# Two-layer convolution and scan network on one Trainium2 core: extra columns that hold the last value of both scans in layer 1

## The chip, the cores and the metric

One core of one Trainium2 chip runs the whole program. The metric is the device time of one execution in microseconds (us).

## The reference, cut to what matters

The input is 32 images of 96 channels and 56 x 56 pixels, in fp32. Layer 0 is a 7 x 7 depthwise convolution, a layer norm over the channels, two dense products with a GELU between them, and a residual sum. Layer 1, where the change is, is a 5 x 5 depthwise convolution followed by a selective scan along the 3136 pixels of each image:

```
x = silu(conv(x) + conv_b);  xs = x.reshape(B, C, L)
x_dbl = einsum('kd,bdl->bkl', x_proj_w, xs)
dts, Bs, Cs = x_dbl[:, :R], x_dbl[:, R:R+N], x_dbl[:, R+N:]
delta = softplus(einsum('dr,brl->bdl', dt_w, dts) + dt_b)
log_dA = maximum(delta * A, log(EPS));  P = exp(cumsum(log_dA))
dB_u = delta * Bs * xs
hs = P * cumsum(dB_u / maximum(P, EPS))
y = einsum('bdnl,bnl->bdl', hs, Cs) + xs * Ds
```

N is 4 (states), R is 6 and EPS is 1e-9.

## The kernel before, in words

The two layers run one after the other, each as a loop over 8 groups of 4 images, and x1_dram holds what goes from one to the other. Each layer is written as one queue of instructions per engine, and the engines are tied by semaphores alone. So every engine does its work in the order of its own queue. The last group of a layer stands as code of its own behind the loop.

In layer 1 the 384 rows of a group (4 images x 96 channels) are three tiles of 128 partitions, and the 3136 pixels are BANDS = 7 bands of BT = 448 columns. A band has STEPS = 12 steps: 3 tiles x 4 states, and a group S = 84 steps. The steps are counted through the group, so that step s is state s % 4 of tile s % 12 // 4 in band s // 12. Bands are counted from 0 here, and the groups too. What happens in one step s:

- ScalarE (ACT) makes d_a = exp(max(delta * A, log EPS)) in two passes, clip_a (L1205) and exp_a (L1211), five steps ahead (DA_LEAD).
- VectorE (DVE) runs a scan with products over d_a, which gives 1 / P in the tile ps_q in PSUM but for its bound (scan_q, L1099; the first value is 1/EPS), cuts it at 1 and multiplies it by u in place (gate, L1115), and runs the scan of the state, h = d_a * h + ps_q (scan_h, L1126). ps_q has two banks and h has six slots (H_SLOTS).
- GpSimd (POOL) makes u = dxs * b_rows (times_b, L1023) three steps ahead, and h = h * c_rows in place (times_c, L1036) one step behind. dxs = delta * xs is made three times per band (times_x, L1011).
- TensorE (PE) adds the four products of a tile in PSUM with matmuls by the identity (add_y, L1348), two steps behind; scan_h waits until the slot that it writes has been added.

A band goes on where the one before it ended, separately in each of the 12 steps. So DVE copies the last column of ps_q to a column of q_last after each scan_q (keep_q, L1107), POOL copies the last column of h to a column of h_last before it overwrites h (L1033), and both scans take that column as their first value 12 steps later. The last band of a group (band 6) has no such copies, since nothing follows it.

```
def keep_q(g, s):
    if b + 1 < BANDS:
        dve.wait_ge(q_done, g * S + s + 1)
        nc.vector.tensor_copy(q_last[:, j:j + 1], ps_q[s % 2][:, BT - 1:BT]).then_inc(q_kept, 1)
```

DVE's queue in step s is keep_q(s), gate(s), at three places of a band sum_delta (L1089), scan_q(s + 1), scan_h(s). sum_delta forms delta of the next band's tile t from ps_prep and z_log at steps 7, 9 and 11 of a band (SUM_AT); it waits for ACT's softplus parts, of which the last is the Ln at L1187.

PE and ACT also prepare the next group's input, spread over the steps by a table (`schedule`, `backs`): transposes of the image (L1293), the banded convolution (L1300), and transposes back to rows of channels (L1313) in bursts at steps 0, 35, 60 and 72, which ACT's SiLU follows (L1169, between two loads of its table of functions). ACT takes all of it out of PSUM: the parts win and conv at L1162. PE waits in its queue for ACT to free the two banks. For the next band PE further has project (L1322) at j = 0 and 1 and delta_rows (L1335) at j = 3, 5 and 7, where j is the step within the band. The last group has none of the preparation. SyncE (SP) issues all DMAs in one queue, among them those of b_rows and c_rows for each band.

Of the kernel before, what the change touches and what calls it, by code (L numbers as in the profile page):

```python
# [81 lines left out]
H_SLOTS = 6  # L82
Y_LAG = 2
# [631 lines left out]
def layer1(nc, groups, x1, t2, consts, out):  # L715
# [4 lines left out]
    with ExitStack() as ctx:  # L720
# [41 lines left out]
        ps_q = [pb(f"ps_q{i}") for i in range(2)]  # L762
        ps_y = [pb(f"ps_y{i}") for i in range(Y_SLOTS)]
        no_q = ps_q[0][:, BT:BT + 1]
# [36 lines left out]
        PREPARED = 4 + TILES + 1  # L801
        S = BANDS * STEPS
        RUNS = BANDS * TILES
        KEPT = (BANDS - 1) * STEPS

# [189 lines left out]
        def _(pool):  # L995
            nc.gpsimd.memset(zeros[:, :], 0.0).then_inc(prepared, 1)
            nc.gpsimd.memset(q_first[:, :], float(np.float32(1) / np.float32(EPS))).then_inc(prepared, 1)
            nc.gpsimd.memset(log_eps[:, 0:1], -LOG_EPS).then_inc(prepared, 1)
            for k in range(Y_SLOTS):
                pool.sem_inc(y_stored[k], 16)  # L1000
# [70 lines left out]
        def _(dve):  # L1071
# [20 lines left out]
            def scan_q(g, s):  # L1092
                b, j = s // STEPS, s % STEPS
                dve.wait_ge(d_a_ready, g * S + s + 1)
                dve.wait_ge(h_done, g * S + max(s, 1))
                if s > 1:
                    dve.wait_ge(q_kept, g * KEPT + min(s - 1, KEPT))  # L1097
                first = q_first[:, 0:1] if b == 0 else q_last[:, j:j + 1]
                nc.vector.tensor_tensor_scan(ps_q[s % 2][:, 0:BT], d_a[s % DA_SLOTS][:, :],  # L1099
                                             no_q.broadcast_to([128, BT]), first,  # L1100
                                             ALU.mult, ALU.add).then_inc(q_done, 1)

            def keep_q(g, s):
                b, j = s // STEPS, s % STEPS
                if b + 1 < BANDS:
                    dve.wait_ge(q_done, g * S + s + 1)
                    nc.vector.tensor_copy(q_last[:, j:j + 1], ps_q[s % 2][:, BT - 1:BT]).then_inc(q_kept, 1)  # L1107

            def gate(g, s):
                b = s // STEPS  # L1110
                dve.wait_ge(q_done, g * S + s + 1)
                if b + 1 < BANDS:
                    dve.wait_ge(q_kept, g * KEPT + s + 1)
                dve.wait_ge(u_done, g * S + s + 1)
                nc.vector.scalar_tensor_tensor(ps_q[s % 2][:, 0:BT], ps_q[s % 2][:, 0:BT], 1.0, u[s % U_SLOTS][:, :],  # L1115
                                               ALU.min, ALU.mult).then_inc(gated, 1)

            def scan_h(g, s):
# [31 lines left out]
        def _(act):  # L1150
# [47 lines left out]
            def clip_a(g, s, first=False):  # L1198
# [70 lines left out]
        def _(pe):  # L1269
# [68 lines left out]
            def add_y(g, s):  # L1338
# [9 lines left out]
                nc.tensor.matmul(total, ident[:, :], h[s % H_SLOTS][:, :],  # L1348
# [119 lines left out]
```

## Time and profile before

| | |
|---|---|
| median of 3 runs | 4020.88 us (4011.57 to 4022.5) |
| the profiled execution's own time | 4020.36 us |
| its span in the trace | 4018.6 us |
| mean granted clock of TensorE | 0.928 |
| first scan of h in layer 1 starts at | 1959.5 us |

Layer 0 takes about the first half of the span; layer 1 holds DVE and POOL at nine tenths in most slices. A row of the trace gives the start in us from the beginning of the span, the duration in us, engine, line, operation, output <- input, shape and count. In brackets stands how long the engine was idle before it and which instruction ended that, as far as the semaphores show. A row's duration is longer than the distance to the next row on the same engine, since the end of one instruction lies over the start of the next; distances between starts tell what an instruction costs.

### The profile page before, as it was taken

How to read it: one execution, taken by the hardware profiler on the slowest of the kernel's cores; microseconds unless marked ns; L12 is line 12 of the kernel's file. 1: busy time of each engine (PE TensorE's matmuls, PEld its weight loads, DVE VectorE, ACT ScalarE, POOL GpSimd, SP SyncE). 2: the span in 40 equal slices, each digit the busy share in tenths (PEclk: the TensorE clock that was granted, in tenths of full speed). 3: DMA queues.
4: the chain of work that ended last, by engine and by line, in shares of the span. 5: the costliest groups of instructions: out<-in, count | busy, mean ns of one | idle time of the engine just before them, and what ended most of it. 6: DMA issues, size and time to landing. Idle time of an engine off the chain costs nothing. (4 is left out here: it accounts for less than half of the span.)

```text
span 4018.6 us, 72697 instructions
## 1 busy us (share of the span) xinstructions
PE 3650.8 (91%) x22358; PEld 2646.6 (66%) x22358; DVE 3106.0 (77%) x4416; ACT 2571.1 (64%) x4292; POOL 2575.8 (64%) x2672
## 2 busy tenths in 40 slices
PE   6999999999999999997899998998989989899776
PEld 6888787979787887877565564664646646466322
DVE  3675758475756667570499998999989989989999
ACT  1463728172735546274688787787778878777754
POOL 0352717162634536270488888888979889888988
PEclk9999999999999999998799898998989989989877
DMA  7546473747465554428565564655546646465222
GB/s 225 170 138 204 104 250 95 251 102 234 109 200 149 164 181 125 149 76 181 130 177 143 162 170 124 172 152 147 164 127 181 169 125 173 129 168 158 86 75 60
DMA packets 383746, 612.84 MB, mean 153 GB/s; under 512 B 199967, under 2 KB 324152, under 8 KB 383048
## 3 DMA queue, kind: packets, MB, share of 16 engines
q1 hardware_dynamic: 383336, 607.74, 53.5%
q8 instruction: 213, 3.49, 0.4%
q14 instruction: 197, 1.61, 0.1%
HBM read 527.35 MB, written 80.28 MB: 151 GB/s over the span
## 5 line engine op out<-in xcount | busy, mean ns | idle before, releaser
L321 POOL TENSOR_TENSOR h_low<-act_h,h_high 128x448 fp32r<-128x448 f32 x448 | 598.0, 1354 | 724.1 <-ACT h_high L520 723.9
L515 ACT ACTIVATE act_h<-ps_up,b 128x448 f32<-128x448 f32 x672 | 408.7, 635 | 728.5 <-PE ps_up L633 728.2
L1348 PE MATMUL ps_y<-h,ident 128*128 128x448 f32 x1344 | 727.1, 629 | 144.3 <-POOL h L1036 113.1
L1036 POOL TENSOR_TENSOR h<-h,c_rows 128x448 f32<-128x448 f32 x672 | 763.7, 1136 | 51.2 <-DVE h L1126 5.7
L1023 POOL TENSOR_TENSOR u<-dxs,b_rows 128x448 f32<-128x448 f32 x672 | 764.5, 1138 | 27.9 <-DVE ps_q L1115 16.8
L1099 DVE TENSOR_TENSOR_SCAN ps_q<-d_a,q_last,ps_q 128x448 f32<-128x448 f32 x576 | 659.5, 1145 | 0.0
L1126 DVE TENSOR_TENSOR_SCAN h<-d_a,h_last,ps_q 128x448 f32<-128x448 f32 x576 | 645.3, 1120 | 0.0
L1300 PEld LDWEIGHTS ps_front<-win,taps 120*112 120x112 f32 x4608 | 540.5, 188 | 149.2 <-issue 147.2
L606 PE MATMUL ps_stage<-win,taps 124*112 124x112 f32 x6144 | 608.3, 261 | 2.7 <-DVE w_low L368 2.7
L606 PEld LDWEIGHTS ps_stage<-win,taps 124*112 124x112 f32 x6144 | 608.1, 178 | 3.2 <-DVE w_low L368 2.8
L1205 ACT ACTIVATE d_a<-delta,log_eps,a_neg 128x448 f32<-128x448 f32 x672 | 503.3, 750 | 114.0 <-DVE h L1126 58.5
L1300 PE MATMUL ps_front<-win,taps 120*112 120x112 f32 x4608 | 543.9, 271 | 5.5 <-ACT win L1162 3.7
L1348 PEld LDWEIGHTS ps_y<-h,ident 128*128 128x128 f32 x1344 | 238.2, 209 | 412.9 <-POOL h L1036 260.3
L1115 DVE SCALAR_TENSOR_TENSOR ps_q<-ps_q,u 128x448 f32<-128x448 f32 x672 | 422.2, 628 | 59.8 <-POOL u L1023 36.1
L426 DVE TENSOR_TENSOR conv<-ps_stage,bias_row 112x448 f32<-112x448 f32 x192 | 179.7, 936 | 350.8 <-PE ps_stage L606 350.8
L1211 ACT ACTIVATE d_a<-d_a 128x448 f32<-128x448 f32 x672 | 387.6, 577 | 8.3
L315 POOL TENSOR_TENSOR ln_rstd<-ln_var,minus_half 112x7 f32<-112x7 f32 x128 | 202.8, 1585 | 285.0 <-DVE ln_var L403 280.9
L1162 ACT ACTIVATE conv<-ps_front 112x448 f32<-112x448 f32 x192 | 181.8, 947 | 214.1 <-PE ps_front L1300 214.1
L629 PE MATMUL ps_up<-hn_high,w_high 96*128 96x448 f32 x672 | 258.4, 385 | 40.3 <-DVE hn_low L413 26.8
L1293 PEld LDWEIGHTS ps_front<-ident,x1pad 32*120 32x120 f32 x2880 | 197.2, 143 | 142.4 <-issue 140.8
L1011 POOL TENSOR_TENSOR dxs<-delta,xs 128x448 f32<-128x448 f32 x168 | 191.1, 1138 | 137.0 <-DVE delta L1089 137.0
L1162 ACT ACTIVATE win<-ps_front 120x480 f32<-120x480 f32 x192 | 203.6, 1062 | 79.9 <-PE ps_front L1293 77.5
(81 smaller groups left out, 6212.6 us busy)
## 6 DMA issues: line engine op xcount, KB each, us to landing
taps<-in_t_dram SPq DMA_DIRECT2D x192, 896.0 KB, 5.0
taps<-in_t_dram SPq DMA_DIRECT2D x192, 672.0 KB, 4.7
b_rows<-bc_dram SPq DMA_DIRECT2D x224, 224.0 KB, 3.0
c_rows<-bc_dram SPq DMA_DIRECT2D x224, 224.0 KB, 3.1
xres<-in_x_dram SPq DMA_DIRECT2D x224, 168.0 KB, 2.5
x_dram<-x1o SPq DMA_DIRECT2D x224, 168.0 KB, 2.0
x1pad<-x_dram SPq DMA_DIRECT2D x96, 392.0 KB, 6.0
out_dram<-y SPq DMA_DIRECT2D x168, 224.0 KB, 2.6
```

What stands on the lines that cost most here:

```text
L321: nc.gpsimd.tensor_tensor(h_low[u % 2][:, t, :], act_h[u % 2][:, t, :], h_high[u % 2][:, t, :], ALU.subtract).then_inc(h_low_ready[t], 1)
L515: nc.scalar.activation(act_h[u % 2][:, t, :], ps_up[t][:, 0:BT], ACT.Gelu, bias=b1[:, t:t + 1]).then_inc(gelu_done, 1)
L606: mm = nc.tensor.matmul(ps_stage[q % 2][0:TOK, c * BLOCKS:(c + 1) * BLOCKS], taps[q % SLOTS1][0:WIN1, c, k, :], win[:, q * CQ + c, :, k:k ...
L1023: nc.gpsimd.tensor_tensor(u[s % U_SLOTS][:, :], dxs[:, t, :], b_rows[n][:, :], ALU.mult).then_inc(u_done, 1)
L1036: nc.gpsimd.tensor_tensor(h[s % H_SLOTS][:, :], h[s % H_SLOTS][:, :], c_rows[n][:, :], ALU.mult).then_inc(hc_done, 1)
L1099: nc.vector.tensor_tensor_scan(ps_q[s % 2][:, 0:BT], d_a[s % DA_SLOTS][:, :], no_q.broadcast_to([128, BT]), first, ALU.mult, ALU.add).then ...
L1115: nc.vector.scalar_tensor_tensor(ps_q[s % 2][:, 0:BT], ps_q[s % 2][:, 0:BT], 1.0, u[s % U_SLOTS][:, :], ALU.min, ALU.mult).then_inc(gated, 1)
L1126: nc.vector.tensor_tensor_scan(h[s % H_SLOTS][:, :], d_a[s % DA_SLOTS][:, :], ps_q[s % 2][:, 0:BT], first, ALU.mult, ALU.add).then_inc(h_d ...
L1205: nc.scalar.activation(d_a[s % DA_SLOTS][:, :], delta[:, t, :], ACT.Relu, bias=log_eps[:, 0:1], scale=a_neg[:, t, n:n + 1]).then_inc(clipp ...
L1211: nc.scalar.activation(d_a[s % DA_SLOTS][:, :], d_a[s % DA_SLOTS][:, :], ACT.Exp, bias=LOG_EPS).then_inc(d_a_ready, 1)
L1300: mm = nc.tensor.matmul(bank[i][0:TOK, c * BLOCKS:(c + 1) * BLOCKS], taps[n % SLOTS2][0:WIN2, c, w, :], win[cb % 2][:, k * CQ + c, :, w:w ...
L1348: nc.tensor.matmul(total, ident[:, :], h[s % H_SLOTS][:, :], start=False, stop=(n == N - 1)).then_inc(y_added, 1)
```

## The change

Instead of a copy in every step, the scans run over columns that carry their last value on.

- **d_a** has two more columns, which are set to 1 once and never written by ACT. **u** has one more, set to 0 once. The ten memsets are on POOL ahead of layer 1's work.
- **scan_q** runs over 450 columns: the two last repeat its last value.
- **gate** runs over 449 columns. It turns column 448 of ps_q into 0 and leaves column 449, which holds the value of scan_q.
- **scan_h** runs over 449 columns: the last repeats h's last value. The slots of h are now one tensor of 6 x 449 columns, so that slots 1, 3 and 5 begin at an odd word. times_c still covers 448 columns, so the extra one is not overwritten.
- **ps_q** is one tensor of two banks. The step's place in a bank begins at column PAIRS - 1 - (s % 12) // 2, that is 5 down to 0, so that each of the six steps that use a bank within a band leaves its kept value one column behind that of the next. One copy of 2 x 6 columns per band then fills q_last.
- **times_c** copies three slots' extra columns to h_last in one instruction, in every third step, and no longer waits between that copy and the product.
- The semaphores q_kept and h_kept count bands and threes of steps; scan_h waits for the copy of the slot that it overwrites.

```diff
+H_KEEP = 3
...
-        d_a = [sb(f"d_a{i}", [128, BT]) for i in range(DA_SLOTS)]
+        d_a = [sb(f"d_a{i}", [128, BT + 2]) for i in range(DA_SLOTS)]
...
-        u = [sb(f"u{i}", [128, BT]) for i in range(U_SLOTS)]
+        u = [sb(f"u{i}", [128, BT + 1]) for i in range(U_SLOTS)]
...
-        h = [sb(f"h{i}", [128, BT]) for i in range(H_SLOTS)]
+        h = sb("h", [128, H_SLOTS, BT + 1])
...
-        ps_q = [pb(f"ps_q{i}") for i in range(2)]
+        ps_q = ctx.enter_context(nc.psum_tensor("ps_q", [128, 2, BANK], F32))
...
+        def q_start(s):
+
+            return PAIRS - 1 - s % STEPS // 2
+
+        def q_bank(s, cols=BT):
+            return ps_q[:, s % 2, q_start(s):q_start(s) + cols]
...
-                if b + 1 < BANDS:
-                    nc.gpsimd.tensor_tensor(h_last[:, s % STEPS:s % STEPS + 1], h[s % H_SLOTS][:, BT - 1:BT],
-                                            zeros[:, 0:1], ALU.add).then_inc(h_kept, 1)
-                    pool.wait_ge(h_kept, g * KEPT + s + 1)
-                nc.gpsimd.tensor_tensor(h[s % H_SLOTS][:, :], h[s % H_SLOTS][:, :], c_rows[n][:, :],
-                                        ALU.mult).then_inc(hc_done, 1)
+                if b + 1 < BANDS and s % H_KEEP == H_KEEP - 1:
+                    j, k = s % STEPS - H_KEEP + 1, s % H_SLOTS - H_KEEP + 1
+                    nc.gpsimd.tensor_tensor(h_last[:, j:j + H_KEEP], h[:, k:k + H_KEEP, BT],
+                                            zeros[:, 0:H_KEEP], ALU.add).then_inc(h_kept, 1)
+                total = h[:, s % H_SLOTS, 0:BT]
+                nc.gpsimd.tensor_tensor(total, total, c_rows[n][:, :], ALU.mult).then_inc(hc_done, 1)
...
-                if s > 1:
-                    dve.wait_ge(q_kept, g * KEPT + min(s - 1, KEPT))
...
+                if b > 0 and j == 0:
+                    dve.wait_ge(q_kept, g * (BANDS - 1) + b)
+                nc.vector.tensor_tensor_scan(q_bank(s, BT + 2), d_a[s % DA_SLOTS][:, :],
...
+            def keep_q(g, b):
+
+                dve.wait_ge(q_done, g * S + (b + 1) * STEPS)
+                nc.vector.tensor_copy(q_last[:, :].rearrange("p (k j) -> p k j", k=2),
+                                      ps_q[:, :, BT + 1:BT + 1 + PAIRS]).then_inc(q_kept, 1)
...
-                if b + 1 < BANDS:
-                    dve.wait_ge(q_kept, g * KEPT + s + 1)
...
+                nc.vector.scalar_tensor_tensor(q_bank(s, BT + 1), q_bank(s, BT + 1), 1.0, u[s % U_SLOTS][:, :],
                                                ALU.min, ALU.mult).then_inc(gated, 1)
...
+                if s >= H_SLOTS:
+                    dve.wait_ge(h_kept, g * (KEPT // H_KEEP) + min(s - H_KEEP, KEPT) // H_KEEP)
+                nc.vector.tensor_tensor_scan(h[:, s % H_SLOTS, :], d_a[s % DA_SLOTS][:, 0:BT + 1], q_bank(s, BT + 1), first,
                                              ALU.mult, ALU.add).then_inc(h_done, 1)
...
-                    keep_q(g, s)
+                    if j == STEPS - 1 and b + 1 < BANDS:
+                        keep_q(g, b)
```

On DVE, steps 9 and 10 of band 0 stand in the queue like this before (SCALAR_TENSOR_TENSOR is also what the list prints for a scan; REGISTER_ALU works out the value of a wait):

```order
L1126 SCALAR_TENSOR_TENSOR h3<-d_a2,zeros,ps_q1 128x448
L1107 COPY q_last<-ps_q0 128x1
L1113 REGISTER_ALU
L1115 SCALAR_TENSOR_TENSOR ps_q0<-ps_q0,u1 128x448
L1094 REGISTER_ALU
L1099 SCALAR_TENSOR_TENSOR ps_q1<-d_a4,q_first,ps_q0 128x448
L1126 SCALAR_TENSOR_TENSOR h4<-d_a3,zeros,ps_q0 128x448
L1107 COPY q_last<-ps_q1 128x1
```

and now:

```order
L1140 SCALAR_TENSOR_TENSOR h<-d_a2,zeros,ps_q 128x449
L1128 SCALAR_TENSOR_TENSOR ps_q<-ps_q,u1 128x449
L1111 REGISTER_ALU
L1115 SCALAR_TENSOR_TENSOR ps_q<-d_a4,q_first,ps_q 128x450
L1140 SCALAR_TENSOR_TENSOR h<-d_a3,zeros,ps_q 128x449
L1122 COPY q_last<-ps_q 128x12
L1128 SCALAR_TENSOR_TENSOR ps_q<-ps_q,u2 128x449
```

The copy between scan_h and the gate is gone from step 10, and the one of step 11 now copies twelve columns for the whole band.

On POOL, steps 14 to 16 stand like this before:

```order
L1033 TENSOR_TENSOR h_last<-h2,zeros 128x1
L1035 REGISTER_ALU
L1036 TENSOR_TENSOR h2<-h2,c_rows2 128x448
L1022 REGISTER_ALU
L1023 TENSOR_TENSOR u0<-dxs,b_rows2 128x448
L1033 TENSOR_TENSOR h_last<-h3,zeros 128x1
L1035 REGISTER_ALU
L1036 TENSOR_TENSOR h3<-h3,c_rows3 128x448
```

and now:

```order
L1051 TENSOR_TENSOR h_last<-h,zeros 128x3
L1054 TENSOR_TENSOR h<-h,c_rows2 128x448
L1039 REGISTER_ALU
L1040 TENSOR_TENSOR u0<-dxs,b_rows2 128x448
L1054 TENSOR_TENSOR h<-h,c_rows3 128x448
```

Ahead of two products in three nothing is left of the copy and its wait.

## Rows read from the trace of the kernel before

**Rows 1.** The page: share of the span busy.
```profile
PE 3650.8 (91%) x22358; PEld 2646.6 (66%) x22358; DVE 3106.0 (77%) x4416; ACT 2571.1 (64%) x4292; POOL 2575.8 (64%) x2672
```

**Rows 2.** POOL's group by line: count, busy us, mean ns, idle before, by whom ended.
```profile
L1033 POOL TENSOR_TENSOR h_last<-h,zeros 128x1 f32<-128x1 f32 x576 | 110.6, 192 | 208.0 <-DMA c_rows<-bc_dram 113.8 <-DVE h L1126 89.3
```

**Rows 3.** DVE in order of time, two steps of band 3 of group 2, the first with a sum_delta.
```profile
2619.97 0.13 DVE L1107 COPY q_last<-ps_q 128x1 f32<-128x1 f32 x1
...
2623.30 0.13 DVE L1107 COPY q_last<-ps_q 128x1 f32<-128x1 f32 x1
2623.47 0.63 DVE L1115 SCALAR_TENSOR_TENSOR ps_q<-ps_q,u 128x448 f32<-128x448 f32 x1
...
2625.07 1.12 DVE L1126 TENSOR_TENSOR_SCAN h<-d_a,h_last,ps_q 128x448 f32<-128x448 f32 x1
2626.11 0.13 DVE L1107 COPY q_last<-ps_q 128x1 f32<-128x1 f32 x1
```

**Rows 4.** DVE in order of time, one step of band 6 of group 2.
```profile
2703.23 0.61 DVE L1115 SCALAR_TENSOR_TENSOR ps_q<-ps_q,u 128x448 f32<-128x448 f32 x1
...
2705.84 0.61 DVE L1115 SCALAR_TENSOR_TENSOR ps_q<-ps_q,u 128x448 f32<-128x448 f32 x1
```

**Rows 5.** DVE in order of time, one step of the last group, band 3.
```profile
3888.27 0.13 DVE L1107 COPY q_last<-ps_q 128x1 f32<-128x1 f32 x1
...
3891.13 0.13 DVE L1107 COPY q_last<-ps_q 128x1 f32<-128x1 f32 x1
```

**Rows 6.** POOL in order of time, one step of group 3 in which it never waits.
```profile
2757.67 0.20 POOL L1033 TENSOR_TENSOR h_last<-h,zeros 128x1 f32<-128x1 f32 x1
2757.94 1.14 POOL L1036 TENSOR_TENSOR h<-h,c_rows 128x448 f32<-128x448 f32 x1
2759.03 1.14 POOL L1023 TENSOR_TENSOR u<-dxs,b_rows 128x448 f32<-128x448 f32 x1
2760.13 0.19 POOL L1033 TENSOR_TENSOR h_last<-h,zeros 128x1 f32<-128x1 f32 x1
```

**Rows 7.** DVE: sum_delta at step 7 of bands 1 to 6, then group 3's band 0.
```profile
2537.20 0.62 DVE L1089 SCALAR_TENSOR_TENSOR delta<-ps_prep,z_log 128x448 f32<-128x448 f32 x1 [1.35 <-ACT z_log L1187]
...
2572.39 0.61 DVE L1089 SCALAR_TENSOR_TENSOR delta<-ps_prep,z_log 128x448 f32<-128x448 f32 x1
...
2608.41 0.62 DVE L1089 SCALAR_TENSOR_TENSOR delta<-ps_prep,z_log 128x448 f32<-128x448 f32 x1 [0.74 <-ACT z_log L1187]
...
2643.63 0.61 DVE L1089 SCALAR_TENSOR_TENSOR delta<-ps_prep,z_log 128x448 f32<-128x448 f32 x1
...
2683.12 0.62 DVE L1089 SCALAR_TENSOR_TENSOR delta<-ps_prep,z_log 128x448 f32<-128x448 f32 x1 [1.96 <-ACT z_log L1187]
...
2717.70 0.62 DVE L1089 SCALAR_TENSOR_TENSOR delta<-ps_prep,z_log 128x448 f32<-128x448 f32 x1 [0.82 <-ACT z_log L1187]
...
2759.14 0.62 DVE L1089 SCALAR_TENSOR_TENSOR delta<-ps_prep,z_log 128x448 f32<-128x448 f32 x1 [0.69 <-ACT z_log L1187]
```

**Rows 8.** ACT: the Ln that the sums of bands 2 and 4 wait for.
```profile
2567.95 0.56 ACT L1187 ACTIVATE z_log<-z_log 128x448 f32<-128x448 f32 x1
...
2639.16 0.56 ACT L1187 ACTIVATE z_log<-z_log 128x448 f32<-128x448 f32 x1
```

**Rows 9.** ACT and PE waits around step 7 of band 4; PE at band 6's burst.
```profile
2644.28 0.76 ACT L1205 ACTIVATE d_a<-delta,log_eps,a_neg 128x448 f32<-128x448 f32 x1 [1.97 <-DVE delta L1089]
...
2648.43 1.86 PE L1348 MATMUL ps_y<-h,ident 128*128 128x448 f32 x2 [1.98 <-ACT win L1162]
...
2700.82 0.64 PE L1348 MATMUL ps_y<-h,ident 128*128 128x448 f32 x1 [1.35 <-POOL h L1036]
```

**Rows 10.** Busy time by stretch of group 2 (PE, PEld, DVE, ACT, POOL; then TensorE's granted clock).
```profile
2530.00:2571.00 41.00, 41.00 (x253) 26.29 (x253) 39.20 (x58) 34.90 (x60) 37.30 (x46) 1.00 0.70 186
2571.00:2586.00 15.00, 13.03 (x71) 8.72 (x69) 14.82 (x23) 9.65 (x18) 13.39 (x17) 0.77 0.46 145
```

**Rows 11.** Line L1126 from first to last: durations in ns, times of its first and last start.
```profile
L1126 DVE TENSOR_TENSOR_SCAN h<-d_a,h_last,ps_q x576: 1118/1120/1148, 2002.0 to 4011.0; 128x448 f32<-128x448 f32 x192
```

More of the change, by code:

```diff
@@ L761, in layer1 @@
         ps_prep = [pb(f"ps_prep{i}") for i in range(2)]
-        ps_q = [pb(f"ps_q{i}") for i in range(2)]
+        ps_q = ctx.enter_context(nc.psum_tensor("ps_q", [128, 2, BANK], F32))
         ps_y = [pb(f"ps_y{i}") for i in range(Y_SLOTS)]
-        no_q = ps_q[0][:, BT:BT + 1]
+        no_q = ps_q[:, 0, BANK - 1:BANK]
         consts_in = sem("consts2_in")
@@ L800, in layer1 @@
         BORDERS = 4
-        PREPARED = 4 + TILES + 1
+        PREPARED = 4 + TILES + 1 + DA_SLOTS + U_SLOTS
         S = BANDS * STEPS
@@ L804, in layer1 @@
         KEPT = (BANDS - 1) * STEPS
+        PAIRS = STEPS // 2
         CONVS = CB // CQ
@@ L871, in z_bank, with q_carry @@
             return ps_prep[(1 + t) % 2]
+        def q_start(s):
+            return PAIRS - 1 - s % STEPS // 2
+        def q_bank(s, cols=BT):
+            return ps_q[:, s % 2, q_start(s):q_start(s) + cols]
+        def q_carry(s):
+            k = s % 2 * PAIRS + q_start(s)
+            return q_last[:, k:k + 1]
         def y_uses(g, r):
@@ L998, in _ @@
             nc.gpsimd.memset(log_eps[:, 0:1], -LOG_EPS).then_inc(prepared, 1)
+            for k in range(DA_SLOTS):
+                nc.gpsimd.memset(d_a[k][:, BT:BT + 2], 1.0).then_inc(prepared, 1)
+            for k in range(U_SLOTS):
+                nc.gpsimd.memset(u[k][:, BT:BT + 1], 0.0).then_inc(prepared, 1)
             for k in range(Y_SLOTS):
@@ L1022, in times_b @@
                     pool.wait_ge(gated, g * S + s - U_SLOTS + 2)
-                nc.gpsimd.tensor_tensor(u[s % U_SLOTS][:, :], dxs[:, t, :], b_rows[n][:, :],
+                nc.gpsimd.tensor_tensor(u[s % U_SLOTS][:, 0:BT], dxs[:, t, :], b_rows[n][:, :],
                                         ALU.mult).then_inc(u_done, 1)
@@ L1095, in scan_q @@
                 dve.wait_ge(h_done, g * S + max(s, 1))
[L1096 to L1107 removed]
+                if b > 0 and j == 0:
+                    dve.wait_ge(q_kept, g * (BANDS - 1) + b)
+                nc.vector.tensor_tensor_scan(q_bank(s, BT + 2), d_a[s % DA_SLOTS][:, :],
+                                             no_q.broadcast_to([128, BT + 2]), q_first[:, 0:1] if b == 0 else q_carry(s),
+                                             ALU.mult, ALU.add).then_inc(q_done, 1)
+            def keep_q(g, b):
+                dve.wait_ge(q_done, g * S + (b + 1) * STEPS)
+                nc.vector.tensor_copy(q_last[:, :].rearrange("p (k j) -> p k j", k=2),
+                                      ps_q[:, :, BT + 1:BT + 1 + PAIRS]).then_inc(q_kept, 1)
             def gate(g, s):
[L1110 removed]
                 dve.wait_ge(q_done, g * S + s + 1)
[L1112 to L1113 removed]
                 dve.wait_ge(u_done, g * S + s + 1)
[L1115 removed]
+                nc.vector.scalar_tensor_tensor(q_bank(s, BT + 1), q_bank(s, BT + 1), 1.0, u[s % U_SLOTS][:, :],
                                                ALU.min, ALU.mult).then_inc(gated, 1)
@@ L1204, in clip_a @@
                     act.wait_ge(h_done, g * S + s - DA_SLOTS + 2)
-                nc.scalar.activation(d_a[s % DA_SLOTS][:, :], delta[:, t, :], ACT.Relu, bias=log_eps[:, 0:1],
+                nc.scalar.activation(d_a[s % DA_SLOTS][:, 0:BT], delta[:, t, :], ACT.Relu, bias=log_eps[:, 0:1],
                                      scale=a_neg[:, t, n:n + 1]).then_inc(clipped, 1)
@@ L1210, in exp_a @@
                 act.wait_ge(clipped, g * S + s + 1)
-                nc.scalar.activation(d_a[s % DA_SLOTS][:, :], d_a[s % DA_SLOTS][:, :], ACT.Exp,
+                nc.scalar.activation(d_a[s % DA_SLOTS][:, 0:BT], d_a[s % DA_SLOTS][:, 0:BT], ACT.Exp,
                                      bias=LOG_EPS).then_inc(d_a_ready, 1)
```

4 lines of the change are left out of this document (1 added, 3 removed).

## The prediction

> **What bounds the kernel now.** I began with the busy shares [rows 1]. PE leads with 91%, but that is a mean over two layers, and the change touches only layer 1. There I asked each engine's order of time how it goes from one step to the next.
>
> DVE runs without a gap through most steps. In a band with copies a step is 2.80 us from one copy to the next, and 3.33 with a sum_delta in between, which so takes 0.53 [rows 3]. Between the copy's start and the gate's lie 0.17 us, between the start of scan_h and the copy's 1.04. Band 6 has no copies, and there the same gate comes again after 2.61 us [rows 4], although the group's preparation still runs beside it. This is the best evidence that there is: the program itself shows the step without its copy. In the last group the step with a copy is longer, 2.86 us [rows 5].
>
> So a band with copies costs DVE 12 x 2.80 + 3 x 0.53 = 35.2 us. Is DVE what bounds a band? The start of sum_delta at step 7 tells that, because there DVE meets the chain of PE and ACT that prepares the next band. In group 2, which I take as the pattern for all seven looped groups, the distances between these starts are 35.2, 36.0, 35.2, 39.5, 34.6 and 41.4 us [rows 7]. In bands 2 and 4 DVE does not wait; the Ln that it needs ended 3.9 us earlier, at 2568.5 and 2639.7 [rows 7, 8]. In all the others DVE waits for ACT. So only two of seven stretches, 1 to 2 and 3 to 4, are bound by DVE alone.
>
> The other stretches belong to PE and ACT. From 2530 to 2571 PE has no idle time at full clock [rows 10]: it is nearly as full as DVE. The chain of 2 to 3 and of 4 to 5 begins where ACT waits 1.97 us for DVE's delta, and PE 1.98 us for ACT in turn [rows 9]; from there to the next step 7 come a burst, SiLUs and the softplus. POOL needs 2.46 us for a step where it does not wait, of which copy and wait are 0.27 [rows 6], and 1.09 for each dxs, by the same row as u: 12 x 2.46 + 3 x 1.09 = 32.8 us a band, less than DVE.
>
> **The change part by part.**
>
> *The copy per step on DVE* (one for each of POOL's 576 [rows 2]) goes, and the step falls from 2.80 to 2.61 us [rows 3, 4]. The copy per band that is left moves twelve columns; a copy of one column costs 0.17 up to the gate [rows 3], and I take the same, 0.2 at most, since eleven columns more at the gate's rate are 0.01. The extra columns: a scan's 1.04 us over 448 columns are 2.3 ns each; the step less the copy and two scans leaves 0.55 for the gate, 1.2 ns each [rows 3], so three scan columns and one gate column add 0.008 us to a step. A band: 12 x 0.19 - 0.17 - 12 x 0.008 = 2.0 us. A band of the last group: 12 x 0.25 - 0.17 - 0.1 = 2.7 us. Band 6 had no copies and pays 0.1 us.
>
> *The copy on POOL* goes in two steps of three, together with its wait: a step falls from 2.46 to 2.19 + 0.27 / 3 = 2.28 us, a band from 32.8 to 30.6. POOL is not the bound, so this counts only where something waits for POOL.
>
> *The ten memsets* come before POOL's first work. Only PE, ACT and POOL wait for them, each ahead of the first band's preparation, and the first group's convolution has to be through before that. At the price of the h_last copy, 0.2 us each [rows 2], they would be 2 us without that cover. I take zero.
>
> *The new waits.* scan_h waits for the h_last copy of three slots, which POOL issues at latest one step after the third; the slot is overwritten at least three steps after that. scan_q waits for the one copy of its band, which is two instructions ahead of it in DVE's own queue. No cost while POOL is under four steps behind.
>
> The sum goes by stretches. **1 to 2 and 3 to 4:** 2.0 us each, and the 3.9 us of slack cover it: 4.0 x 7 groups = 28. **Last group:** it has no preparation, so all six bands with copies are DVE's: 6 x 2.7 = 16. **5 to 6:** PE waits 1.35 us for POOL's product at the burst of band 6 [rows 9], after POOL ran without waiting for some ten steps; POOL gains 0.18 a step, which is more than 1.35 in all. Behind that PE's own work binds: 1.3 x 7 = 9. **2 to 3:** the whole chain starts earlier together with DVE's delta, and its length, 36.0, is PE's and ACT's. Lower bound of the gain 0. But this chain starts with PE's idle 2 us. Around that wait in band 2 the granted clock is 0.77 over 15 us [rows 10], a mix of the two levels 1.2 and 2.4 GHz, and the add behind the same wait in band 4 takes 1.86 us [rows 9], where the full clock's is about 1.0. DVE comes 2.0 us earlier and takes just that idle time away. If the clock then stays at 2.4 GHz, 0.23 x 15 = 3.4 us of PE time come back and DVE binds again at 33.2: upper bound 2.8. I see nothing that settles it and take half: 1.4 x 7 = 10. **0 to 1, 4 to 5, and 6 to the next band 0:** PE and ACT, or the turn of the loop; 0 (at 4 to 5 up to 3 by the same clock). Band 6: -0.1 x 8 = -1.
>
> Sum: 28 + 16 + 9 + 10 - 1 = 62 us. The profiled execution took 4020.4, half a us under the median of the runs, so 3958.
>
> On the clock, the Trainium skill (TensorE: Matmul & The Clock Gate, "What's actually happening") says that the array runs at half rate after an idle spell and at full rate after sustained work. The trace agrees in so far as 0.77 stands behind the wait and 1.00 over the stretch without idle time [rows 10]. By that rule the 2 to 3 term would be its upper bound, 20 us in place of 10, and the time 3948.
>
> **The rivals.**
>
> *All bands follow DVE.* With its idle time gone PE keeps the full clock everywhere, and ACT's waits shrink too. Then 42 looped bands give 2.0 each: 84 + 16 - 1 = 99, time 3921. For it: DVE, PE and ACT wait on one another in a ring, and shorter DVE steps shorten the ring. Against: in five of seven stretches DVE waits for ACT now, and nothing in the change makes ACT or PE do less.
>
> *PE binds the free bands too.* In the stretch from 1 to 2 PE is 100% busy [rows 10] and waits only behind its end, by the same 2 us; if its busy time does not pack any tighter than that, or the clock falls elsewhere, these bands give 0.7 instead of 2.0, and 2 to 3 gives nothing: 10 + 16 = 26, time 3994. For it: rows 10. Against: the matmuls' ends are modelled, and slack of 3.9 us at ACT's Ln.
>
> *Odd words, small.* Slots 1, 3 and 5 of h begin at an odd word, and so does ps_q in half the steps. No row of this trace has a wide operand of DVE or POOL there. If the gate alone took a fifth longer, 0.11 us in every second step, a step would gain 0.13 instead of 0.19: the DVE terms shrink by a third, time about 3980. The Trainium skill (Vector Engine (DVE) Microarchitecture Reference, "Measured stream behaviour on trn2") gives 1.30 ns per column in place of 1.05 where pairs of words start on an odd word while both sources hop. No run here shows it; our streams are contiguous, where it would touch only the ends.
>
> *Odd words on POOL: slower.* POOL's product reads and writes h in place. If it takes twice its 1.09 us in the three odd slots, a band costs POOL 30.6 + 6 x 1.09 = 37.1 us, in every band of every group. Now a band costs 36.5 on average (2009 us for 55 bands [rows 11]), so POOL would bind the kernel: 55 x 0.6 = 33 us more, and up to a further 60 if half of its 114 us of waits for c_rows stays [rows 2]: about 4080. It turns slower where the odd product passes 1.09 + (35.2 - 30.6) / 6 = 1.9 us. Against: POOL's rows give 2.4 ns a column, slow enough to hide a second fetch.
>
> *The copy is not what it costs.* If the 0.17 us were the gap of any two dependent instructions, removing the copy would save nothing. Band 6 speaks against it clearly, with scan_h followed straight by the gate; this has no chance of its own.
>
> **How the numbers follow.** The forecast has 0.58 (its own range 3940 to 3975, by the 2 to 3 term's bounds and the clock's). All bands follow: 0.15. PE binds: 0.12. Odd words small: 0.08. Slower: 0.07. Leaving out the last and a little at the other end, the range is 3918 to 3995. A measurement of this kernel can tell about 0.3%, 12 us, from no change. Slower by over that: 0.07; within it, from the tails of the third and fourth cases: 0.05; faster: 0.88.
>
> **What would show it right or wrong.** DVE's gate-to-gate distance of 2.62 us in every band, with no copy but one per band. POOL's step 2.19 without a copy. sum_delta distances of 33.2 at 1 to 2 and 3 to 4, near 39 to 41 at 4 to 5 and 6 to 0; the last group's bands 33.2 instead of 35.9. ACT's and PE's waits of 2 us [rows 9] gone or under 0.3, and TensorE's clock behind them: 1.00 would carry the 2 to 3 term, 0.77 would not. The prediction is wrong if wide gates or products at odd slots are longer than at even ones, if stretches 4 to 5 and 6 to 0 shrink as well (then I called a ring a chain), or if the free bands do not reach 33.2.

## The result

The changed kernel takes 3964.4 us (median of 4 runs, 3962.8 to 3967.5), the kernel before 4021.7 (4 runs): ratio 0.9856, 95% interval 0.9832 to 0.9881, some 57 us. The forecast was 3958. The same kernel run again in a later session stood at 0.9817 (0.9796 to 0.9838), 3961.5 against 4032.5. The profiled execution took 3967.5 us.

Of the page, the busy shares [rows 1], and of the groups by line the two copies that are left:

```profile
PE 3632.9 (92%) x22358; PEld 2638.3 (67%) x22358; DVE 3026.1 (76%) x3888; ACT 2572.0 (65%) x4292; POOL 2459.8 (62%) x2298
...
L1051 POOL TENSOR_TENSOR h_last<-h,zeros 128x3 f32<-128x3 f32 x192 | 37.8, 197 | 76.5 <-DMA c_rows<-bc_dram 50.0 <-DVE h L1140 26.2
...
L1122 DVE COPY q_last<-ps_q 128x12 f32<-128x12 f32 x48 | 6.9, 144 | 0.0
```

DVE has 528 instructions fewer, POOL 374, and both copies take nearly as long as those of one column did. DVE in order of time, around the end of band 3 of group 2, answers to [rows 3, 4]; the last three rows are of the last group [rows 5]:

```profile
2607.84 0.61 DVE L1128 SCALAR_TENSOR_TENSOR ps_q<-ps_q,u 128x449 f32<-128x449 f32 x1
2608.36 1.15 DVE L1115 TENSOR_TENSOR_SCAN ps_q<-d_a,q_last,ps_q 128x450 f32<-128x450 f32 x1
2609.41 1.13 DVE L1140 TENSOR_TENSOR_SCAN h<-d_a,h_last,ps_q 128x449 f32<-128x449 f32 x1
2610.45 0.14 DVE L1122 COPY q_last<-ps_q 128x12 f32<-128x12 f32 x1
2610.51 0.62 DVE L1128 SCALAR_TENSOR_TENSOR ps_q<-ps_q,u 128x449 f32<-128x449 f32 x1
...
3848.76 0.61 DVE L1128 SCALAR_TENSOR_TENSOR ps_q<-ps_q,u 128x449 f32<-128x449 f32 x1
3849.28 0.61 DVE L1106 SCALAR_TENSOR_TENSOR delta<-ps_prep,z_log 128x448 f32<-128x448 f32 x1
...
3851.91 0.61 DVE L1128 SCALAR_TENSOR_TENSOR ps_q<-ps_q,u 128x449 f32<-128x449 f32 x1
```

Gate to gate is 2.67 us with the copy of twelve columns in between. The copy starts 0.06 us before the gate, where the copy of one column started 0.17 before it. The likely difference is the wait: before, the gate waited for its copy (q_kept), now nothing right behind the copy does. No run has the one-column copy without its wait. Where DVE does not wait, steps without it are 2.61 to 2.64 in every band, the last group's too. The last group's two gates are 3.15 apart with a sum_delta between them, which takes 0.53 from start to start, so 2.62 without.

The starts of sum_delta (DVE forms the next band's delta) at step 7, in group 2 from band 1 on [rows 7]:

```profile
2530.47 0.62 DVE L1106 SCALAR_TENSOR_TENSOR delta<-ps_prep,z_log 128x448 f32<-128x448 f32 x1 [1.79 <-ACT z_log L1202]
...
2563.58 0.61 DVE L1106 SCALAR_TENSOR_TENSOR delta<-ps_prep,z_log 128x448 f32<-128x448 f32 x1
...
2599.39 0.62 DVE L1106 SCALAR_TENSOR_TENSOR delta<-ps_prep,z_log 128x448 f32<-128x448 f32 x1 [2.69 <-ACT z_log L1202]
...
2632.49 0.61 DVE L1106 SCALAR_TENSOR_TENSOR delta<-ps_prep,z_log 128x448 f32<-128x448 f32 x1
...
2671.41 0.62 DVE L1106 SCALAR_TENSOR_TENSOR delta<-ps_prep,z_log 128x448 f32<-128x448 f32 x1 [2.71 <-ACT z_log L1202]
...
2706.49 0.62 DVE L1106 SCALAR_TENSOR_TENSOR delta<-ps_prep,z_log 128x448 f32<-128x448 f32 x1 [1.96 <-ACT z_log L1202]
...
2747.02 0.62 DVE L1106 SCALAR_TENSOR_TENSOR delta<-ps_prep,z_log 128x448 f32<-128x448 f32 x1 [1.10 <-ACT z_log L1202]
```

The distances of all looped groups, read in the same way from both profiles and added up, tell where the time came from (us; below them what was forecast). The turn from the seventh group into the last, 35.3 before and 33.3 after, is not in the column 6 to 0, since the last group has no preparation:

| stretch between step 7 of bands | 0 to 1 | 1 to 2 | 2 to 3 | 3 to 4 | 4 to 5 | 5 to 6 | 6 to 0 | last group, six bands |
|---|---|---|---|---|---|---|---|---|
| one, before | 35.2 to 40.6 | 35.2 | 35.2 to 36.2 | 35.2 | 36.8 to 40.9 | 34.4 to 34.6 | 39.9 to 41.4 | |
| one, after | 36.2 (once 38.3) | 33.1 | 35.8 | 33.1 | 38.8 to 38.9 | 35.1 | 40.2 to 40.5 | |
| gain in all | 14 | 15 | 1 | 15 | -3 | -4 | 4 | 17 |
| forecast | 0 | 14 | 10 | 14 | 0 | 9 | 0 | 16 |

Against these 59 us, layer 1 reached its first step 7 6 us later than in the profile of before. That point lies between 1981 and 1985 us in the profiles of this study without the ps_q change and between 1979 and 1989 in those with it (with PE's work cut at 1970 and 1975), so these 6 us are within its spread.

### The profile page after: what moved, and what is told of

The parts are those of the page before. It is cut to its first block, busy times and chain, and to the rows that moved or that the text cites. A ratio compares the mean times of both kernels' runs of the same rounds, so it can differ in the third digit from the quotient of the medians.

```text
span 3965.7 us, 71069 instructions
## 1 busy us (share of the span) xinstructions
PE 3632.9 (92%) x22358; PEld 2638.3 (67%) x22358; DVE 3026.1 (76%) x3888; ACT 2572.0 (65%) x4292; POOL 2459.8 (62%) x2298
## 4 chain that ended last, share of the span: by engine, by line
PE 40%; issue 6%; ACT 3%; POOL 2%; DVE 2%; DMA 0%; DVEq 0%; ACTq 0%; POOLq 0%
PE ps_front L1315 12%; PE ps_y L1363 12%; PE ps_front L1308 4%; PE ps_prep L1337 4%; PE ps_y L1360 3%; PE ps_prep L1350 3%; PE ps_front L1328 2%; DVE h L1140 1%; POOL h L1054 1%; POOL u L1040 1%; DVE ps_q L1115 1%; ACT win L1177 1%; ACT d_a L1226 1%; ACT xs L1184 1%; POOL dxs L1028 1%
## 5 line engine op out<-in xcount | busy, mean ns | idle before, releaser
L1054 POOL TENSOR_TENSOR h<-h,c_rows 128x448 f32<-128x448 f32 x672 | 728.1, 1084 | 219.5 <-DVE h L1140 141.2
L1363 PE MATMUL ps_y<-h,ident 128*128 128x448 f32 x1344 | 704.8, 612 | 104.9 <-POOL h L1054 92.0
L1040 POOL TENSOR_TENSOR u<-dxs,b_rows 128x448 f32<-128x448 f32 x672 | 762.1, 1134 | 51.9 <-DMA bc_dram<-xd 37.6
L1115 DVE TENSOR_TENSOR_SCAN ps_q<-d_a,q_last,ps_q 128x450 f32<-128x450 f32 x576 | 661.2, 1148 | 0.2 <-ACT d_a L1226 0.2
L1140 DVE TENSOR_TENSOR_SCAN h<-d_a,h_last,ps_q 128x449 f32<-128x449 f32 x576 | 647.0, 1123 | 0.0
L1128 DVE SCALAR_TENSOR_TENSOR ps_q<-ps_q,u 128x449 f32<-128x449 f32 x672 | 409.4, 609 | 42.3 <-POOL u L1040 42.0
L1106 DVE SCALAR_TENSOR_TENSOR delta<-ps_prep,z_log 128x448 f32<-128x448 f32 x168 | 103.6, 617 | 216.3 <-ACT z_log L1202 210.4
```

The source lines that it names most:

```text
L1040: nc.gpsimd.tensor_tensor(u[s % U_SLOTS][:, 0:BT], dxs[:, t, :], b_rows[n][:, :], ALU.mult).then_inc(u_done, 1)
L1054: nc.gpsimd.tensor_tensor(total, total, c_rows[n][:, :], ALU.mult).then_inc(hc_done, 1)
L1115: nc.vector.tensor_tensor_scan(q_bank(s, BT + 2), d_a[s % DA_SLOTS][:, :], no_q.broadcast_to([128, BT + 2]), q_first[:, 0:1] if b == 0 els ...
L1128: nc.vector.scalar_tensor_tensor(q_bank(s, BT + 1), q_bank(s, BT + 1), 1.0, u[s % U_SLOTS][:, :], ALU.min, ALU.mult).then_inc(gated, 1)
L1140: nc.vector.tensor_tensor_scan(h[:, s % H_SLOTS, :], d_a[s % DA_SLOTS][:, 0:BT + 1], q_bank(s, BT + 1), first, ALU.mult, ALU.add).then_inc ...
L1363: nc.tensor.matmul(total, ident[:, :], h[:, s % H_SLOTS, 0:BT], start=False, stop=(n == N - 1)).then_inc(y_added, 1)
```

## The experiments

**The two halves, each alone.** First the ps_q half; h and its copy stay as they were.

```diff
-        h = sb("h", [128, H_SLOTS, BT + 1])
+        h = [sb(f"h{i}", [128, BT]) for i in range(H_SLOTS)]
...
+                if b + 1 < BANDS:
+                    nc.gpsimd.tensor_tensor(h_last[:, s % STEPS:s % STEPS + 1], h[s % H_SLOTS][:, BT - 1:BT],
+                                            zeros[:, 0:1], ALU.add).then_inc(h_kept, 1)
+                    pool.wait_ge(h_kept, g * KEPT + s + 1)
```

> The ps_q half of the change alone: extra columns in d_a, u and ps_q, one copy to q_last per band; h and its copy in every step on GpSimd as before. Theory A (DVE's copy is the whole gain): DVE's step 2.61 us in bands 0 to 5, the stretches 1 to 2 and 3 to 4 at 33.1, POOL's step back at 2.46, and a time within 8 us of the changed kernel (3964), since POOL needs 32.8 us a band and DVE 33.1. Rival B (GpSimd's shorter step is needed too): with POOL at 32.8 plus its waits it becomes the bound behind each wait for c_rows, the free stretches stay near 34 and the time is 3985 or more. If the wait of PE for POOL's product at the burst of band 6 comes back (about 1.3 us), the stretch 5 to 6 should be back at 34.5 from 35.1.

3976.1 us, ratio 0.9875 (0.9838 to 0.9912). DVE's step is 2.61 and the stretches 1 to 2 and 3 to 4 are 33.1, so theory A holds. The time is 12 us over the 3964 of the whole change, outside the 8 expected, but the kernel before also stood 7 us higher beside this run (4028.7); by the ratios, 0.9875 and 0.9856, the distance is 8 us, and the two intervals overlap. Its profile has 0 to 1 at 40.5 to 40.7 in three of seven groups, where the changed kernel has 36.2, and that is 11 us. The stretch 5 to 6 came back to 34.5, as expected. PE at band 6's burst in this run, group 2, with its wait for POOL's product [rows 9] ahead:

```profile
2686.28 1.02 PE L1362 MATMUL ps_y<-h,ident 128*128 128x448 f32 x2 [1.35 <-POOL h L1054]
2687.13 0.93 PE L1327 MATMUL ps_front<-ident,conv 112*128 112x112 f32 x8
2688.41 1.13 PE L1327 MATMUL ps_front<-ident,conv 112*128 112x112 f32 x8 [0.34 <-ACT xs L1183]
2689.73 1.13 PE L1327 MATMUL ps_front<-ident,conv 112*128 112x112 f32 x8 [0.20 <-ACT xs L1183]
```

and in the changed kernel:

```profile
2690.91 1.13 PE L1328 MATMUL ps_front<-ident,conv 112*128 112x112 f32 x8 [1.33 <-ACT xs L1184]
2692.23 3.30 PE L1328 MATMUL ps_front<-ident,conv 112*128 112x112 f32 x16 [0.20 <-ACT xs L1184]
```

With a shorter POOL step PE no longer waits for POOL, but it comes to the burst only to wait 1.33 us for ACT's first SiLU, and behind that 16 records take 3.30 us, where 8 take 1.13 at full clock. The wait changed its owner, and the clock fell within the burst. The granted clock of the whole stretch 5 to 6 of group 2 was 1.00 in the kernel before and in this run; in the changed kernel it was 0.95, and 0.57 over these 4 us:

```profile
2671.40:2706.50 35.10, 33.44 (x160) 19.83 (x159) 33.14 (x41) 31.50 (x52) 33.15 (x34) 0.95 0.32 102
2692.00:2696.00 4.00, 3.80 (x18) 2.76 (x18) 4.00 (x5) 3.04 (x6) 4.00 (x4) 0.57 0.02 6
```

Then the h half alone; ps_q and its copy in every step stay.

```diff
-                    if j == STEPS - 1 and b + 1 < BANDS:
-                        keep_q(g, b)
+                    keep_q(g, s)
```

> The h half alone: h in one tensor with an extra column, one copy to h_last per three steps; ps_q and its copy in every step on DVE as before. Theory A: DVE's step stays 2.80 us, the free stretches 35.2, and the time stays within 10 us of the kernel before (4021). Rival B (GpSimd's copy and its wait held the chain up): 15 us or more faster than before. The last group tells the third thing: if its step of 2.86 us comes from DVE's own code it stays; if it came from GpSimd's copies it falls to 2.80.

4019.6 us, ratio 0.9976 (0.9953 to 0.9999). The free stretches are 35.2 and the last group's step stays 2.86: theory A. Against the kernel before beside it (4028.7) that is 9 us, and the interval leaves between 0 and 19, so the copy on GpSimd was worth little but not surely under 10. The 2.86 come from DVE's own code. The two halves' gains, 1.25% and 0.24%, add up to the 1.44% of the whole change within their intervals.

**PE's work cut, in both kernels.** One window of three is left in the preparation's convolution. Two of three of its matmuls are left out, so the output is not the reference's and only the time is read:

```diff
-                        for w in range(KT2):
+                        for w in range(1):
```

> The kernel before with one window of three in the convolution of layer 1's preparation (two of three matmuls on L1300 left out, so the convolution is not the reference's), the partner of the next run. PE loses some 0.8 us in each of 8 pieces a band, 6 us of about 32. Theory A (PE's full queue held DVE in the stretches 0 to 1, 2 to 3 and 4 to 5): DVE binds nearly everywhere, the step-7 distances are 35.2 in 0 to 1, 1 to 2, 2 to 3 and 3 to 4. Rival B (ACT's bursts and the softplus hold them whatever PE does): 2 to 3 stays near 36.0 and 4 to 5 at 37 to 39.

> The changed kernel with the same two of three matmuls left out. Theory A: all four stretches from 0 to 4 at 33.1, and the distance to the run before this is what the change would give with PE out of the way: 2.1 us in each of 42 looped bands and 2.85 in six of the last group, near 100 us, against 57 measured with the whole of PE's work. Rival B: as little as with the whole work, 55 to 65 us.

3989.4 us without the change, ratio 0.9893 (0.9853 to 0.9933), and 3896.7 with it, ratio 0.9657 (0.9617 to 0.9696): 93 us apart. sum_delta at step 7 of bands 2 and 3, group 2, with the change:

```profile
2540.33 0.60 DVE L1106 SCALAR_TENSOR_TENSOR delta<-ps_prep,z_log 128x448 f32<-128x448 f32 x1
...
2573.36 0.60 DVE L1106 SCALAR_TENSOR_TENSOR delta<-ps_prep,z_log 128x448 f32<-128x448 f32 x1
```

33.03 us, no wait; the whole kernel has 35.8 and a wait of 2.7. Without the change the same stretch is 35.2 in all groups. Theory A for 2 to 3: with two thirds of that convolution out of PE's queue it gives 15 us in place of 1, and 5 to 6 gives 9 in place of -4. Of the four stretches expected at 33.1, 0 to 1 falls short with 34.3 to 37.8. The two profiled executions are only 73 us apart, since they are the fastest and the slowest of their four runs, and 4 to 5 and 6 to 0 gave 2 and -2 us, so the 93 are not to be read as the expected 100 all but reached. What the changed kernel leaves unused at 2 to 3 and 5 to 6 is held by PE's work.

**PE's order at the bursts.**

```diff
+                    if burst:
+                        for i in burst[:2]:
+                            back(g if s == 0 else g + 1, i)
                     if s >= Y_LAG:
                         add_y(g, s - Y_LAG)
                     if burst:
-                        for i in burst:
+                        if s > 0:
+                            for t in projects:
+                                project(f, fb, t)
+                        for i in burst[2:]:
                             back(g if s == 0 else g + 1, i)
```

> The changed kernel with PE's order at the bursts altered: two transposes back first, then add_y and (at steps 60 and 72) the two project products, then the other transposes, so that the wait for ACT's first SiLU (1.72 us at steps 35 and 60, 1.33 at 72) has work over it. Theory A (stretches 2 to 3, 4 to 5 and 5 to 6 are bound by PE's and ACT's chain, its idle time and its clock): 2 to 3 falls by 0.8, 4 to 5 from 38.9 by 1.7 and by up to 2 more if the clock stays at its upper level, 5 to 6 by about 1; together 3 to 5 us a group, time 3935 to 3945. Rival B (DVE's delta and POOL hold these stretches): no change within 5 us.

3945.4 us, ratio 0.9792 (0.9761 to 0.9823). TensorE's clock and busy time (PE, PEld, DVE, ACT, POOL, then the clock, the DMA share and GB/s) over the stretch 4 to 5 of group 2, in this run in two pieces:

```profile
2632.60:2650.00 17.40, 16.21 (x106) 11.10 (x105) 17.40 (x22) 14.68 (x23) 13.06 (x13) 1.00 0.94 200
2650.00:2667.00 17.00, 17.00 (x96) 11.47 (x96) 14.88 (x19) 15.02 (x27) 12.66 (x14) 1.00 0.69 212
```

and in the changed kernel:

```profile
2632.50:2671.40 38.90, 36.14 (x209) 24.98 (x208) 33.33 (x41) 30.67 (x50) 26.00 (x27) 0.91 0.72 180
```

The stretch is 35.3 here and 36.6 to 37.2 in five of the seven groups, against 38.9. But 2 to 3 did not move (35.8) and 5 to 6 hardly (34.6 to 35.2), so theory A holds for the large burst alone. The second time, beside the changed kernel on the same chip:

> The changed kernel once more, unaltered, beside the next three on the same chip. It should stand at 0.9856 of the kernel before, within 0.003, and have its step-7 distances again: 36.2 in 0 to 1 (40.5 where the granted clock over that stretch is 0.78 instead of 0.86), 33.1, 35.8, 33.1, 38.9, 35.1.

> The changed kernel with work laid over the waits at the bursts, once more. If its gain was real: 4 to 5 near 36.6 instead of 38.9 in most groups, and the time 12 to 25 us under the run before this one, with intervals of the two ratios that do not meet. If it was the clock's luck in 0 to 1, under 8 us.

3961.5 us, ratio 0.9817 (0.9796 to 0.9838), and 3949.6 us, ratio 0.9792 (0.9772 to 0.9811). The changed kernel came 0.004 below the 0.9856 expected, outside the 0.003 allowed, so ratios of different sessions carry that much doubt; its stretches came again as expected. 4 to 5 is 35.5 to 37.0 again. The medians are 12 us apart, but the intervals meet, where they were expected not to: 0 to 1 is 39.0 in three groups of the altered order's profile where the changed kernel has 36.2. It may be a version that beats both; its gain of 2 to 3 us a group in one stretch is shown, its gain in the whole time is not settled. In the kernel before:

> The kernel before with PE's order at the bursts altered as in the run on the changed kernel that gained about 19 us. Theory A (the bursts are PE's and ACT's chain in both kernels): 2 to 3 and 4 to 5 shorten here too, 10 to 25 us in all, time 3997 to 4012, and the change and the order add up. Rival B (the bursts became the bound only through the change): under 5 us, time 4016 or more.

4028.4 us, ratio 0.9991 (0.9965 to 1.0017): nothing. In the profile 4 to 5 gave 9 us in all, mostly where it had been 39 and more (three groups were at 36.8 already), but 5 to 6 rose from 34.5 to 35.1 and 6 to 0 grew by 4.5 us in all, which took it back. So rival B is right by the time and not by the stretch: the large burst was PE's and ACT's chain here too.

**Latency or throughput.**

```diff
                     pieces = schedule[s] if more else []
+                    if (more or b + 1 < BANDS) and j in DELTA_AT:
+                        delta_rows(f, fb, DELTA_AT.index(j))
```

> The changed kernel with PE's delta_rows ahead of the preparation's piece in the same step (steps 3, 5 and 7 of a band), about 1.2 us earlier, with the same work in all. Theory A (throughput: PE's queue is full): 2 to 3 stays at 35.8 and 4 to 5 at 38.9 within 0.5, the time within 6 us of the changed kernel. Rival C (latency: DVE waits for the softplus of the next band, and that for delta_rows): 2 to 3 falls by 0.8 or more, as do 4 to 5 and 5 to 6, 15 us or more in all.

3992.9 us, ratio 0.9909 (0.9888 to 0.9931), so 31 us slower than the changed kernel beside it. No expectation foresaw that. Locally rival C is right for the most part: 2 to 3 falls from 35.8 to 34.6 in five groups, though it rises to 37.6 in two, 5 to 6 from 35.1 to 33.1, 4 to 5 by 0.6 in most. So these stretches are not held by PE's throughput alone; 1.2 us earlier in the queue is worth 1 to 2 us. But 6 to 0 went from 40.4 to 42 and more, and 0 to 1 to 41.4 in four groups (42.5 in one). The busy time and clock over three stretches 0 to 1 of this run:

```profile
2243.20:2278.50 35.30, 33.05 (x202) 20.89 (x201) 33.23 (x40) 28.01 (x47) 32.46 (x34) 0.95 0.67 197
2492.80:2534.20 41.40, 40.16 (x217) 25.17 (x218) 33.34 (x41) 28.37 (x47) 33.55 (x35) 0.79 0.58 170
2752.40:2793.80 41.40, 40.15 (x218) 25.20 (x218) 33.34 (x40) 28.37 (x47) 33.70 (x35) 0.79 0.58 168
```

The same stretch in the kernel before (two groups) and in the changed one:

```profile
2496.70:2537.20 40.50, 40.50 (x213) 25.12 (x212) 35.00 (x52) 28.40 (x47) 36.68 (x45) 0.78 0.58 171
2759.10:2794.30 35.20, 33.88 (x204) 21.51 (x203) 34.74 (x51) 29.05 (x49) 34.18 (x43) 0.95 0.68 192
```

```profile
2494.20:2530.40 36.20, 35.97 (x202) 21.96 (x200) 33.24 (x40) 28.04 (x47) 34.41 (x37) 0.86 0.66 195
```

DVE and ACT do nearly the same in the rows of one kernel, TensorE has 9 to 16 records more in the long ones. The length goes with the granted clock: 0.95 for 35, 0.86 for 36, 0.78 for 41 us. The product of TensorE's busy time and clock is 31 to 32 us in all of them, so in the long ones TensorE is busy nearly throughout at a lower clock. Both alterations together:

> Both alterations together. Theory A: as the altered bursts alone, within 6 us. Rival C: the gains of both add up.

3961.1 us, ratio 0.9819 (0.9799 to 0.9839): no better than the change alone, and 11 us over the altered bursts alone, so neither theory's number came (within 6 us, or both gains).

**Where the operands lie.** h slots 450 columns apart instead of 449:

> As the changed kernel, but with h slots 450 columns apart, so that all begin at an even word. In the changed kernel GpSimd's product takes 0.98 us in slots 2 and 3 and 1.14 us in the other four. If odd words mattered, the new durations would split by the parity of the slot or become all equal. If it is the distance in bytes from something else (slots 2 and 3 lie 8 and 12 bytes past the places of slots 448 columns apart), the fast slots should be 1 and 2 or thereabouts (8 bytes a slot: 8 and 16). The time should stay within 5 us of 3964, since GpSimd does not bind.

3969.1 us in one run. GpSimd's product h * c_rows takes 0.98 us in slots 1, 3 and 5 and 1.14 in the others. The split goes by slot parity, but all slots now begin at even words, and the expected slots 1 and 2 were wrong. What fits both layouts is the place within 16 bytes, counted from slot 0: offset 8 or 12 is fast (with 449 columns slots 2 and 3, with 450 the odd ones), 0 or 4 is not. So h and b_rows were both moved by 8 bytes:

```diff
-        h = sb("h", [128, H_SLOTS, BT + 1])
+        h = sb("h", [128, H_SLOTS, BT + 4])[:, :, 2:BT + 3]
-        b_rows = [sb(f"b_rows{i}", [128, BT]) for i in range(N)]
+        b_rows = [sb(f"b_rows{i}", [128, BT + 2])[:, 2:BT + 2] for i in range(N)]
```

> The changed kernel with PE's order at the bursts altered, and with the starts of h's slots and of b_rows moved by two words (8 bytes), the h slots 452 columns apart so that all are alike. If GpSimd's product is faster where one input starts 8 or 12 bytes into a line of 16 and the other at its head, both products take 0.98 us in place of 1.14 in every slot, u as well as h times c. If it is the output that has to be shifted, only the h product (written in place) is at 0.98 and u stays at 1.13. The time: within 6 us of the altered order alone (3945), since GpSimd has 2.5 us to spare in a band; it may help behind the waits for c_rows.

3963.4 us, ratio 0.9812 (0.9766 to 0.9858), with the altered bursts in it. POOL in order of time:

```profile
2534.30 0.98 POOL L1054 TENSOR_TENSOR h<-h,c_rows 128x448 f32<-128x448 f32 x1 [3.95 <-DVE h L1140]
2535.24 1.14 POOL L1028 TENSOR_TENSOR dxs<-delta,xs 128x448 f32<-128x448 f32 x1
2536.33 0.99 POOL L1040 TENSOR_TENSOR u<-dxs,b_rows 128x448 f32<-128x448 f32 x1
```

Both products take 0.98 in every step; dxs, whose inputs were not moved, stays at 1.14. For u only an input was moved, so it is an input's place that counts and not the output's. Whether it is the place itself or the distance to the other input's is open, since no run moved both. It brings no time: the median is even 14 to 18 us above the altered bursts alone, outside the 6 expected but inside overlapping intervals, with 0 to 1 at 40.4 to 40.5 in three groups again.

## Why the prediction was right

The sum was right to 6 us, but several of its terms were not, and their errors cancel. DVE's step was right. "A step falls from 2.80 to 2.61" is what band 6 had shown, and it held in all bands; the odd words cost nothing on DVE, and on POOL the product became faster in slots 2 and 3, of which only slot 3 begins at an odd word. The copy per band was sized at 0.17 and costs 0.06, probably since most of the 0.17 had been the gate's wait for its copy; the free band is 33.1 (33.0 in the last group) instead of 33.2.

The two free stretches (28, measured 29) and the last group (16, measured 17) carry the result as forecast. The slack at the Ln [rows 8] was the right sign of a free band. DVE's 2.1 us in 42 looped bands and the last group would have been near 100 us, against 59; the pair with PE's work cut shows that some 28 of the missing 40 were held by PE's work at 2 to 3 and 5 to 6. For the rest it shows nothing, since 0 to 1, 4 to 5 and 6 to 0 gave only 6 us together there.

The step on 2 to 3 failed: "the whole chain starts earlier together with DVE's delta". PE and ACT in the changed kernel, group 2, beside [rows 9]:

```profile
2564.26 0.75 ACT L1220 ACTIVATE d_a<-delta,log_eps,a_neg 128x448 f32<-128x448 f32 x1
2565.83 0.95 ACT L1177 ACTIVATE conv<-ps_front 112x448 f32<-112x448 f32 x1 [0.82 <-PE ps_front L1315]
...
2569.33 1.63 PE L1363 MATMUL ps_y<-h,ident 128*128 128x448 f32 x2 [0.84 <-ACT win L1177]
```

ACT no longer waits for delta, but PE's wait shrank only to 0.84 us and PE starts again 5.8 us behind sum_delta, not the 4.8 of before (2572.39, and 2577.20 for PE in the same view): ACT now waits 0.82 us for PE's convolution instead. The clock over 15 us there rose from 0.77 to 0.89:

```profile
2563.00:2578.00 15.00, 14.16 (x83) 9.59 (x84) 15.00 (x21) 11.85 (x21) 13.14 (x14) 0.89 0.46 139
```

That shortened the rest of the chain from 31.2 to 30.1 us, and the two cancel: 35.8 for 36.0, a gain of 1 where 10 were forecast and 20 were the upper bound. The clock rose as forecast, and its worth went elsewhere. Where it went, TensorE's work in the stretches 1 to 2 and 2 to 3 of group 2 shows, first before, then in the changed kernel:

```profile
2537.20:2572.39 35.19, 35.19 (x217) 22.63 (x218) 34.77 (x51) 29.22 (x50) 31.35 (x40) 1.00 0.64 176
2572.39:2608.41 36.02, 32.33 (x195) 21.17 (x193) 34.86 (x53) 29.13 (x46) 32.96 (x41) 0.91 0.62 171
```

```profile
2530.47:2563.58 33.11, 33.11 (x202) 21.05 (x203) 33.11 (x40) 28.50 (x49) 27.96 (x30) 1.00 0.66 183
2563.58:2599.39 35.81, 33.26 (x208) 22.06 (x206) 33.12 (x41) 29.91 (x48) 31.68 (x33) 0.95 0.63 171
```

In the free stretch PE is busy without a gap at full clock, before and after. When DVE shortens it by 2.1 us, PE gets less done: 12 matmuls of the convolution, which take 1.34 us at full clock, move into the next stretch. So the moved work takes up 1.3 us, nearly what the clock gave back: an estimated 1.4 us, 0.04 of 36, by 0.95 for 0.91. At 3 to 4 and 4 to 5 the same 12 matmuls move, and in the three groups where 4 to 5 had been 36.8, the gain of 3 to 4 is lost whole: both stretches together are 72.0 us before and after. Where the clock stays up, the moved work does fit: in the first group of the run with the shifted operands (and the altered bursts) the stretch 2 to 3 has a granted clock of 1.00 and takes 33.6 us with 207 records, near the prediction's 33.2.

The step on 5 to 6 failed too, and in sign: 9 forecast, -4 measured. I had taken the wait for POOL's product as the gate of the burst. The ps_q half alone, set beside the whole change, shows that it hid ACT's lateness: with the wait for POOL gone, PE waits 1.33 us for ACT's SiLU instead of 0.34, and the granted clock of the stretch is 0.95 in place of 1.00.

Two terms that were put at zero were not: 0 to 1 gave 14 and 6 to 0 gave 4. Of the four groups of before at 40.5 none is left in the changed kernel's first profile. In it, in its repetition and in the layout of 450 columns the stretch is 36.2 in 18 of 21 groups; the repetition and the other layout each have one group at 40.6 to 40.7. That the length goes with the clock is shown; why the clock stays up there is not. So the sum was right partly by luck: these 18 us stand in for the 22 that failed at 2 to 3 and 5 to 6.

No rival came true as a whole. "PE binds the free bands too" was right that 2 to 3 gives nothing and that PE is full in the stretch ahead, and wrong that the free bands give only 0.7. "All bands follow DVE" was not reached even with PE's work cut: there 1 to 2, 2 to 3 and 3 to 4 follow DVE, and 0 to 1 and 6 to 0 do not. One of the prediction's own signs of being wrong came up in part: 6 to 0 shrank, though 4 to 5 did not.

## What to carry to other kernels

If one band of a loop lacks an operation, its step is the best price of that operation. What the price is worth is read per stretch, from the slack at the place where the engine meets the others' chain. A stretch that one engine frees can be taken back in the next one, if another engine was full in it: look for the work that moves. A copy was dear here where the next instruction waited for it: twelve columns without that wait cost 0.06 us, one column with it 0.17. With PE's queue nearly full, every reordering here moved the clock as well; judge a reordering by the whole time over several runs, not by the stretch that it shortens.

## What the runs showed of the hardware that was not expected

- GpSimd's product of two 128 x 448 fp32 operands takes 0.98 us instead of 1.14 when one input begins 8 or 12 bytes further within 16 bytes than before, the other staying. It was so in the slots concerned in three layouts (slots 449, 450 and 452 columns apart).
- DVE's step in the last group, whose code stands behind the loop, was 2.86 us with a copy and 2.61 without, in the loop 2.80 and 2.61: the dependent copy was 0.06 us dearer there. Why stays open.
- With nearly the same work of DVE and ACT, the stretch 0 to 1 takes 35 us at a granted clock of 0.95 and 41 at 0.78, from group to group of one execution. Three such groups are 11 us, as much as most differences between the later versions. Runs of one kernel spread in the same sense: in one session the kernel before took 4014.7 us at a mean clock of 0.933 and 4058.0 at 0.920. Which stretches make that up is known for the profiled executions only.
